# GpSimd waits for each indirect transfer to land before it issues the next

## The reference, cut to what matters

```python
x = x + 0.5 * _L0_ffn_ref(_layernorm(x), ...)   # layer l=0: 8 experts, each token takes 2, one shared expert
x = x + _L0_attn_ref(_layernorm(x), ...)        # linear attention, group norm
x = x + 0.5 * _L0_ffn_ref(_layernorm(x), ...)   # the same ffn again: l=1
x = x + 0.5 * _L1_ffn_ref(_layernorm(x), ...)   # top-1 of 8 small experts, gelu
x = x + _L1_attn_ref(_layernorm(x), ...)        # gated linear recurrence
x = x + 0.5 * _L1_ffn_ref(_layernorm(x), ...)
```

## Time and profile before

| | |
|---|---|
| median of three runs | 1219.88 us |
| span of the profiled execution | 1611.3 us |
| mean granted TensorE clock in it | 0.851 |
| GpSimd (POOL) busy | 645.2 us, 40% |
| TensorE (PE) / VectorE (DVE) / ScalarE (ACT) busy | 1208.2 / 1037.9 / 881.7 us |

### The profile page before, as it was taken

One profiled execution on the slowest core, in us unless ns is written; L12 is line 12 of the kernel. 1 busy time (PEld: TensorE's weight loads), 2 busy tenths in 40 slices (PEclk: granted clock), 3 DMA queues, 4 the chain that ended last, 5 costly groups with the idle time before them and its releaser, 6 DMA issues.

```text
span 1611.3 us, 37336 instructions
## 1 busy us (share of the span) xinstructions
PE 1208.2 (75%) x14084; PEld 950.7 (59%) x14113; DVE 1037.9 (64%) x3441; ACT 881.7 (55%) x1505; POOL 645.2 (40%) x679
## 2 busy tenths in 40 slices
PE   3745767567766778767666766799989897989997
PEld 2423545455555666555554645677877676768776
DVE  7954655455645656666664664677767757888774
ACT  3545556334544445645543653676677445766764
POOL 1364443344555455555545453431322323342100
PEclk9876878787887978988887887898898978999989
DMA  8012323223132322222132222311210101010001
GB/s 263 14 50 62 79 68 75 59 63 83 57 84 70 78 71 76 62 65 55 57 87 67 68 67 66 76 43 46 56 46 23 28 18 33 15 29 24 2 9 34
DMA packets 172875, 93.77 MB, mean 58 GB/s; under 512 B 98516, under 2 KB 163183, under 8 KB 172575
## 3 DMA queue, kind: packets, MB, share of 16 engines
q1 hardware_dynamic: 115886, 35.64, 9.0%
q0 software_dynamic: 16384, 33.59, 7.3%
q10 hardware_dynamic: 40432, 22.17, 4.9%
HBM read 25.78 MB, written 45.61 MB: 44 GB/s over the span
## 4 chain that ended last, share of the span: by engine, by line
PE 37%; DVE 22%; ACT 13%; another core or an unknown queue 13%; issue 12%; POOL 1%; DMA 1%; ACTq 0%; POOLq 0%; DVEq 0%; SPq 0%
PE bank L759 8%; PE bank L581 3%; PE bank L820 2%; PE bank L967 2%; PE bank L806 2%; PE bank L839 2%; DVE x L1135 2%; PE bank L775 2%; PE sums L984 1%; PE sums L901 1%; PE bank L532 1%; PE sums L904 1%; ACT heads_store L1674 1%; DVE heads_store L1189 1%
## 5 line engine op out<-in xcount | busy, mean ns | idle before, releaser
L1914 POOL DMA_INDIRECT rows<-store,r_slot x256 | 258.8, 1011 | 185.1 <-DVE r_slot L1396 114.1
L759 PE MATMUL bank<-u_xp,w_hi 128*128 128x128 f16 x2432 | 267.3, 237 | 83.7 <-issue 74.0
L1930 POOL DMA_INDIRECT y_in<-ys,r_result x256 | 262.2, 1024 | 120.6 <-issue 70.3
L759 PE MATMUL bank<-u_xp,w_lo 128*128 128x128 f16 x1216 | 245.7, 237 | 34.6 <-issue 34.4
L759 PEld LDWEIGHTS bank<-u_xp,w_hi 128*128 x2432 | 212.3, 108 | 100.0 <-issue 94.4
L759 PEld LDWEIGHTS bank<-u_xp,w_lo 128*128 x1216 | 130.3, 107 | 47.1 <-issue 47.1
L581 PE MATMUL bank<-heads_store,w_hi 128*128 128x512 f16 x256 | 92.6, 449 | 7.0 <-DVE r_lg L1164 4.2
L1874 POOL TENSOR_SCALAR ve_last<-mv_last 128x4 f32<-128x4 f32 x16 | 3.1, 195 | 215.0 <-DVE mv_last L1092 214.9
L1698 ACT ACTIVATE heads_store<-bank,sc 128x512 f32<-128x512 f32 x64 | 43.3, 682 | 75.0 <-PE bank L581 41.1
L1135 DVE SCALAR_TENSOR_TENSOR x<-y_in,r_weight,x 128x128 f32<-128x128 f32 x256 | 72.5, 346 | 1.1
L1189 DVE TENSOR_TENSOR heads_store<-bank,heads_store 128x512 f32<-128x512 f32 x64 | 43.7, 686 | 42.7 <-ACT heads_store L1698 33.9
(11 more groups left out here) (434 smaller groups left out, 3478.4 us busy)
## 6 DMA issues: line engine op xcount, KB each, us to landing
ys<-u_y_even ACTq DMA_DIRECT2D x38, 256.0 KB
ys<-u_y_odd ACTq DMA_DIRECT2D x38, 256.0 KB
u_xp<-rows SPq DMA_TRANSPOSE x304
x<-x_dram SPq DMA_DIRECT2D x16, 256.0 KB, 5.6
rows<-store,r_slot POOLq DMA_INDIRECT x256
y_in<-ys,r_result POOLq DMA_INDIRECT x256
out_dram<-x SPq DMA_DIRECT2D x16, 256.0 KB
rows<-blank SPq DMA_DIRECT2D x48, 64.0 KB
```

Of the source, the lines that this page charges most:

```text
L759: ins = pe.matmul(B[:, of_block[j]], of_expert(wp, e, F16, part, which), xp_rows[:, xp, of_block[j]], start=(n == 0 and j == 0), stop=(n = ...
L1914: pool.indirect_dma_start(row_dram[g], bass.IndirectOffsetOnAxis(route.slot[g][:, i, t:t + 1].bitcast(U32), 0), rows[:, groups[g].first * ...
L1930: pool.indirect_dma_start(fetch.y[i][:, t, k, :], None, y_dram[g], bass.IndirectOffsetOnAxis(route.result[g][:, k, t0 + t:t0 + t + 1].bitc ...
```

## The change

`pool_program` gets a list with at most one entry: the semaphore, and the value that it has when the transfer issued last has landed. Ahead of each scatter and each fetch GpSimd waits for that entry, and puts the entry of the coming transfer in its place. So a transfer is issued only when the one before it has landed, also where a scatter follows a fetch. The powers between transfers don't wait for it, but those that stand behind a transfer in the queue stand behind its wait too.

```diff
         def pool_program(pool):
             on = Waiting(pool)
+            in_flight = []
+
+            def previous_landed(landing, value):
+                if in_flight:
+                    on.wait_ge(*in_flight.pop())
+                in_flight.append((landing, value))
...
                 for i in range(2):
+                    previous_landed(scattered[g], 16 * (2 * groups[g].tiles * l + 2 * t + i + 1))
                     pool.indirect_dma_start(
                         row_dram[g], ...).then_inc(scattered[g], 16)
...
+                previous_landed(fetched[i], 16 * (2 * T * (l * (chunks // 2) + c // 2) + n + 1))
                 pool.indirect_dma_start(
                     fetch.y[i][:, t, k, :], None, y_dram[g], ...).then_inc(fetched[i], 16)
```

## The result

The changed kernel takes 1825.67 us (median of four runs, 1818.43 to 1833.60). The kernel before, recorded beside it, takes 1219.86 us. The ratio is 1.496, with a 95% interval from 1.490 to 1.502: much slower, as forecast, but outside the range of 1500 to 1800 us. The added time is 606 us, where 440 were forecast.

The account below looks back on a forecast made before the run. Three compute engines and their waits bound the kernel before; afterwards GpSimd's transfers would. 50 us, 1057 us of transfers and 75 us of waits gave 1182 to the last scatter; plus 440 and 40 made 1662, said as 1660; range 1500 to 1800.

Parts of the forecast that it names:

- What bounds the kernel: Before the change, TensorE, VectorE, ScalarE and their waits set the time; GpSimd follows, with 359 us of slack from 58 to 980 us.
- Even stretching (factor 0.757): Scales the 1611.3 us profile evenly to the runs: scatters end at 742 us, and 478 us are left behind them.
- in proportion to TensorE's instructions: Other reading: 230 of the 391 us excess lie behind the last scatter; scatters end at 819 us, 401 us follow.
- My addition of 40 us for powers behind longer bursts: Behind the last scatter, powers wait behind bursts of 7 or 8 fetches: 13 bursts x 3 us = 40 us.
- a last stretch 80 us longer: Sign of being wrong: the time behind the last scatter growing by over 80 us; it should keep its length within 10%.
- I take 2.45, the mean of the three rounded: Period of a scatter that waits for landing, from three clean cases: 2.45 us, between 2.17 and 2.67; 1.18 us more than before.
- 2.85 for a fetch: Period of a fetch that waits for landing, from one landing: 2.85 us, between 2.52 and 2.99; 1.58 us more than before.
- The residual waits: GpSimd's waits for other engines left up to the last scatter after the change: 75 us, a fifth of 359.
- The other number: Same terms on the unscaled profile: about 58 + 1057 + 75, then 631 + 40, a span near 1860 us.
- The slack takes it: Rival: GpSimd's 359 us of slack absorb most of 541 us added, 182 show: 1400 us; 9 in 100 for 1260 to 1500.
- Nothing is absorbed: Rival: each of 488 transfers in bursts pushes everything, 675 us more: 1895 us; 7 in 100 for more than 1800.
- No more than before: Rival: the chain's 13% unnamed waits are landings held up by overlapping transfers; one at a time frees 159 us: 1061 us; 2 in 100.

Follow-up runs that it names:

- old_wait: Kernel before plus, ahead of each GpSimd transfer, a wait that is always met: 1222.79 us beside 1223.19 on one chip, 1577.6 beside 1584.3 on another.
- split_free: Kernel before with scatters' and fetches' semaphores split into even and odd ones, no wait for a landing: 1613.0 us, ratio 1.001.

## Why the prediction was wrong

*What bounds the kernel.* Partly wrong. That GpSimd has room was read from a trace in which the other engines were held up. On the quick chip it had 58 us of such waits up to the last scatter, 22 of them ahead of the first, not 359.

*The first step that failed: "Even stretching (factor 0.757): in a run the middle stretch ends at 742 us and what is left takes 478 us. Or in proportion to TensorE's instructions".* The longer profiled execution was the same kernel with stalls in it, and these are not spread like time or like instructions. They lie beside GpSimd's bursts: by the traces of `old_wait` and of before, the last scatter was at 680 and 977 us, and 540 and 634 us lay behind it. So 297 of the 391 us are up to the last scatter and 94 behind. I gave the last stretch 401 to 478 us; it takes 540. The changed kernel's stands at 594, against my 440 + 40. That is 114 us of error in a forecast that was 160 us short in sum. My addition of 40 us for powers behind longer bursts was about right against 540 + 54: VectorE waited 50 us for powers behind the last scatter, where it had waited 9. I had named a last stretch 80 us longer as a sign of being wrong; against my own 401 to 478 us it is 116 to 193 longer, against the 540 it is 54.

*The second: "I take 2.45, the mean of the three rounded", and 2.85 for a fetch.* Mechanism right, size low, and as costly as the first. The distances have medians of 2.58 and 2.89 us, near what I took; but their means are 2.82 for a scatter and 3.02 for a fetch, because landings spread upwards, to 5.0 us (mean 2.50 for a scatter with a median of 2.29, and 2.75 for a fetch with one of 2.62). Powers are hidden but for about 0.1 us each, as I had it: between two scatters the mean is 2.81 us without a power and 2.95 with one. Why some landings are slow is open. Up to the last scatter it is (1227.55 - 58.47) / 404 = 2.89 us for each, where I had 1057 / 407 = 2.60 (three of my 151 fetches come behind the last scatter): 112 us more. A few clean cases give the usual landing; the sum needs the mean.

*The residual waits.* 75 us were put in; 22 us came before the first scatter, where they were counted already, and 4 behind it. These 75 us too many hid most of the previous error, and that is luck. The first scatter came 8.5 us later than my 50. So the last scatter was forecast at 1182 us and started at 1227.6.

*The sum of the errors.* 112 + 8.5 - 75 + 114.5 = 160 us, and 1662 + 160 = 1822, the span measured.

*The other number.* The span of "near 1860 us" that I gave for a profiled execution was much the better forecast (1822), since it scaled nothing, but it was right by two errors that partly cancel: 1190 for 1228 us up to the last scatter, 671 for 594 behind.

*The rivals.* "The slack takes it" fell with the slack: 182 us should have shown, and 606 did. "Nothing is absorbed" (1895 us, 7 in 100) came nearest (1826), and up to the last scatter it describes the quick chip best: of GpSimd's waits for others only some 30 us were there to absorb, beside 547 us added. Behind the last scatter it doesn't: 54 us came for 107 fetches. The profile after gives 2.3 and 2.6 us from issue to landing. The fit of the Trainium skill (DMA: Bandwidth & Descriptors, section "Anatomy of one DMA — SWDGE (gpsimd) path"), with the 2.15 us and 1480 us estimated from it, was further off than the rows; the measurement decides. "No more than before" was wrong for this change, but not in kind. On a stalling chip close transfers do go with stalls of other engines, and 1.43 us instead of 1.28 between two gives 8% back; only 2.9 us costs far more than there is to get.

## What to carry to other kernels

When the profiled execution is a third longer than the timed runs, don't scale it; find the idle time with no named releaser, see beside what it lies, and take it out there, as it may be hiding the engine that is next to bound the time. An engine that issues transfers is full when the distance between their starts, times their number, fills the stretch together with its other work, whatever its busy share says; a wait for each landing turns that distance from the time of an issue into that from issue to landing and waking, and a mean over many, not the usual case, is what multiplies by 404. And where the same program has different times on different chips, compare only kernels that ran side by side.

## What the runs showed of the hardware

- The same program took 1223 us on one chip and 1584 to 1614 us on four others. Each chip came up at one time only, so that it is the chip is not shown. In the trace of before, while GpSimd issued indirect transfers 1.26 us apart in bursts, ScalarE stood for up to 20.0 us, VectorE for up to 12.4 and TensorE's matmuls for up to 8.6 with no releaser named, and SyncE took 16.71 us for eight issues. What holds them is open. It isn't which semaphores the transfers raise (`split_free`), nor a lack of instructions between them (`old_wait`). A larger median distance between transfers lessens it: 413 to 500 us of such waits of ScalarE and VectorE at 1.28 us, 255 to 343 at 1.43, 49 at 1.76, 3 at 2.31. Overlap lessens with distance: by the 2.3 us of a scatter's landing, an estimated 1.8 are in flight at 1.28 us and 1.0 at 2.31, so overlap may be the cause as well as distance.
- A scatter of 128 rows of 512 bytes from SBUF to DRAM by index took 2.3 us from issue to landing in the median, 2.5 in the mean and 5.0 at most, and the next started 2.49 us behind it at the earliest; a fetch of as much took 2.6 in the median, and the next started at 2.69 us at the earliest.
- TensorE's mean granted clock was 0.96 up to the last scatter in `old_wait`, where it was busy for 538 of 622 us, and 0.75 in the changed kernel, where it was busy for 619 of 1172; behind it 0.98 and 0.92. TensorE's busy time behind it is 510 for 494 us, so the clock may have part in the 54 us that the last stretch grew; no run separates it from the waits for powers.
